# The layer norm of the streamed last stage: root on VectorE, normalising one step earlier

## Chip, core and metric

The kernel runs on one core of one Trainium2 chip. The metric is the device time of one launch in microseconds (us): 2959.16 us before the change, the median of three runs (2955.97, 2959.16 and 2968.11). About 0.5% of it, some 15 us, is what a measurement of this kernel can tell from no change.

## The reference, cut to what matters

A decoder of four levels; the change touches only the last stage, `L3_ffn`: six layers (DEPTH) over x of 4 x 256 x 128, each of local attention with 16 heads of 64 and a gated feed-forward part behind a layer norm.

```python
def ffn_layer(x, g, bln, W1, b1, W2, b2):
    mu = x.mean(-1, keepdims=True)
    var = ((x - mu) ** 2).mean(-1, keepdims=True)
    xn = (x - mu) / jnp.sqrt(var + 1e-05) * g + bln
    hg = xn @ W1 + b1
    a, gate = jnp.split(hg, 2, -1)
    return a * jax.nn.gelu(gate, approximate=False) @ W2 + b2
for i in range(DEPTH):
    x = attn_layer(shift_tokens(x), Wqkv[i], q_scale[i], k_scale[i], Wo[i]) + x
    x = ffn_layer(shift_tokens(x), ln_g[i], ln_b[i], W1[i], b1[i], W2[i], b2[i]) + x
```

`shift_tokens` moves the upper 64 columns of each row one token down.

## The kernel before

The stage is one block, `stream`, that runs all six layers without a barrier. Its unit is the **job**, one batch of one layer: JOBS = 24 jobs, each of 8 (PER) **groups**, a group being a pair of heads. The program walks through **ticks** s, and every engine has its own loop over the same ticks. In each tick the engines do one step each for groups of different age: TensorE scores group s (L2076, L2081), turns q and k of group s + 1 (L2093), turns the probabilities of group s - 2 (`flip`, L2102) and sums the values of group s - 3 (L2199); VectorE takes the row maxima (L2376) and ScalarE the exponentials (L2233). What a job needs once is put at fixed ticks after its first group. I count a job's ticks from there: the output projection stands at OUT = 12, the shifted late rows at LATE = 13, the turn of the normalised rows at ZT = 15, the gates at 16, and so on to DOWN = 19. So the norm of job n runs while the groups of the next job are worked on. In even ticks TensorE projects q of a future job (L2054), in odd ones k (L2063) and v (L2068), up to tick 183 of the whole stage (its groups end at tick 191).

Each engine takes its instructions strictly in the order in which the code's loops write them. So the place of a step in an engine's loop decides what stands behind it. The places that matter here:

- VectorE, tick 13, last: the copy of the late half into z (`late_moved`, L2424). Tick 14: first the reciprocal of the sums of the group before (L2359, POOL waits for it), then `bn_stats`, `bn_aggr` and two small operations that leave variance + eps in `ln_sum` (L2371) and minus the mean in `ln_shift` (L2372), and only then the row maxima of the tick's group (L2376). Later in the tick come two products for the rotation (L2346, L2352), the copy of the turned probabilities, and in even ticks the copy of the next group's `qk_T`. 
- POOL, tick 14: shares out the probabilities (L2305), scales the next group (L2315), then the inverse root of the norm (`inverse_root`, L1861 to L1867: 14 small operations that wait for each other, by Newton steps from a bit trick) and `ln_shift` times `ln_inv` (L2325), then L2297, which adds the two parts of the rotation.
- ScalarE, tick 13, last: the lower half of z (`low_moved`, L2247). Tick 15, last: it waits for `ln_shifted`, normalises the two tiles of z (L2259), waits for their transpose and moves it to `znT` (L2263). The first thing of every tick is the copy of the values that TensorE has summed into `rope` (`stored`, L2217), since they share PSUM bank 7 with the v projection.
- TensorE, tick 15: k projection, v projection, scores, turn, flip, then the two transposes of z (L2143, waits for `normed`), then the values.

The v projection waits for that copy at the top of the same tick on ScalarE:

```python
until(pe, stored, min(G, s - VALUES))
until(pe, v_copied, u)
nc.tensor.matmul(v_bank, own, w_qkv[:, 2 * INNER + c * BANK:2 * INNER + (c + 1) * BANK],
```

Of the kernel before, what the change touches and what calls it, by code (L numbers as in the profile page):

```python
# [16 lines left out]
I32 = mybir.dt.int32  # L17
ALU = mybir.AluOpType
# [3 lines left out]
P = 128  # L22
# [3 lines left out]
QT = N // P  # L26
# [18 lines left out]
LN_EPS = 1e-5  # L45
# [59 lines left out]
def decoder(nc, a, out):  # L105
    ctx = ExitStack()
    with ctx:
        signal = Signals(nc, ctx, [(name, 1) for name in AHEAD] + [(name, STEPS_AHEAD) for name in AHEAD_BY_STEPS])
# [10 lines left out]
        def copy(engine, dst, src, scale=1.0):  # L119

            if engine == "act":
                return nc.scalar.activation(dst, src, ACT.Copy, scale=scale)  # L122
            if isinstance(scale, float) and scale == 1.0:
                return nc.vector.tensor_copy(dst, src)  # L124
            return nc.vector.tensor_scalar(dst, src, scale, None, ALU.mult)

        def affine(engine, dst, src, scale, bias):

            if engine == "act":
                return nc.scalar.activation(dst, src, ACT.Identity, bias=bias, scale=scale)  # L130
            return nc.vector.tensor_scalar(dst, src, scale, bias, ALU.mult, ALU.add)
# [3 lines left out]
        xin = sb("xin", [P, NT, D])  # L135
        z = sb("z", [P, NT, D])
        xnT = sb("xnT", [P, T])
        stats = sb("stats", [P, MT, 6])
# [1647 lines left out]
        def l3_ffn():  # L1786
            sub = ExitStack()
            with sub:
                def sbl(name, shape, dt=F32):
                    return sub.enter_context(nc.sbuf_tensor("net_" + name, shape, dt))  # L1790
# [17 lines left out]
                ln_sum, ln_inv, ln_shift, ln_temp = sbl("ln_sum", [P, QT]), sbl("ln_inv", [P, QT]), sbl("ln_shift", [P, QT]), sbl("ln_temp", [P, 3, QT])  # L1808
# [14 lines left out]
                with nc.Block() as block:  # L1823
# [8 lines left out]
                    def _(pool):  # L1832
# [4 lines left out]
                       (head_sums, head_inv, head_temp), (ln_sum, ln_inv, ln_shift, ln_temp), (qk_T, probs, flat_p, maxima, sums, inverse, window16),  # L1837
# [32 lines left out]
        def stream(p, GT, rows, weights, tables, heads_norm, ln, softmax, ffn):  # L1870
# [18 lines left out]
            ln_sum, ln_inv, ln_shift, ln_temp = ln  # L1889
# [9 lines left out]
            half = D // 2  # L1899
# [15 lines left out]
            measured, gathered, spread_in = signal("net_measured", 2 * JOBS), signal("net_gathered", 2 * JOBS), signal("net_spread", 2 * JOBS)  # L1915
            ln_rooted, normed = signal("net_ln_rooted", ROOT_OPS * JOBS), signal("net_normed", 2 * JOBS)
# [13 lines left out]
            def at_tick(s, lag, every, count):  # L1930

                i, rest = divmod(s - lag, every)
                return i if rest == 0 and 0 <= i < count else None

            def job(n):
                return n // B, n % B
# [15 lines left out]
            def half_cols(c):  # L1952
                return slice(c * BANK, (c + 1) * BANK)
# [20 lines left out]
            with ps("bank", [P, 8, BANK]) as bank, nc.Block() as block:  # L1974
# [229 lines left out]
                def _(act):  # L2204
# [7 lines left out]
                    for s in TICKS:  # L2212
# [9 lines left out]
                        if u is not None:  # L2222
                            m, c, t = step_of(u)
                            square(u, 1, k_filled)
                            act.wait_ge(v_filled.sem, v_filled.at(0, u + 1))
                            copy("act", vals[:, m % 3, t, half_cols(c)], v_bank).then_inc(v_copied.sem, 1)
                        g = s
# [14 lines left out]
                        n = at_tick(s, LATE, PER, JOBS)  # L2242
                        if n is not None:
                            l, b = job(n)
                            own = slice(QT * b, QT * (b + 1))
                            act.wait_ge(out_added.sem, out_added.at(0, n + 1))
                            copy("act", z[:, own, 0:half], xin[:, own, 0:half]).then_inc(low_moved.sem, 1)  # L2247
# [5 lines left out]
                        n = at_tick(s, ZT, PER, JOBS)  # L2253
                        if n is not None:
                            l, b = job(n)
                            act.wait_ge(ln_shifted.sem, ln_shifted.at(0, n + 1))
                            for q in range(QT):
                                own = z[:, QT * b + q, :]
                                affine("act", own, own, ln_inv[:, q:q + 1], ln_shift[:, q:q + 1]).then_inc(normed.sem, 1)  # L2259
                            if b == 0:  # L2260
                                act.wait_ge(ffn_in.sem, ffn_in.at(l, FFN_LOADS))
                            act.wait_ge(z_turned.sem, z_turned.at(0, n + 1))
                            affine("act", znT[:, :], spare[:, 0:N], vec[:, 0:1], vec[:, 1:2]).then_inc(z_moved.sem, 1)  # L2263
# [16 lines left out]
                def _(pool):  # L2280
# [19 lines left out]
                    for s in TICKS:  # L2300
# [19 lines left out]
                        n = at_tick(s, LATE + 1, PER, JOBS)  # L2320
                        if n is not None:
                            pool.wait_ge(spread_in.sem, spread_in.at(0, 2 * n + 2))
                            inverse_root(pool, ln_sum[:, :], LN_EPS, ln_inv[:, :], ln_temp, ln_rooted, ROOT_OPS * n)
                            pool.wait_ge(ln_rooted.sem, ln_rooted.at(0, ROOT_OPS * (n + 1)))
                            nc.gpsimd.tensor_tensor(ln_shift[:, :], ln_shift[:, :], ln_inv[:, :], ALU.mult).then_inc(ln_shifted.sem, 1)  # L2325
# [11 lines left out]
                def _(dve):  # L2337
# [16 lines left out]

                    for s in TICKS:
# [4 lines left out]
                        n = at_tick(s, LATE + 1, PER, JOBS)  # L2360
                        if n is not None:
                            l, b = job(n)
                            dve.wait_ge(late_moved.sem, late_moved.at(0, n + 1))
                            dve.wait_ge(low_moved.sem, low_moved.at(0, n + 1))
                            for q in range(QT):
                                nc.vector.bn_stats(stats[:, q, :], z[:, QT * b + q, :]).then_inc(measured.sem, 1)
                            for q in range(QT):
                                dve.wait_ge(measured.sem, measured.at(0, 2 * n + q + 1))
                                nc.vector.bn_aggr(meanvar[:, q, :], stats[:, q, :]).then_inc(gathered.sem, 1)
                            dve.wait_ge(gathered.sem, gathered.at(0, 2 * n + 2))  # L2370
                            nc.vector.tensor_scalar(ln_sum[:, :], meanvar[:, 0:QT, 1], LN_EPS, None, ALU.add).then_inc(spread_in.sem, 1)  # L2371
                            nc.vector.tensor_scalar(ln_shift[:, :], meanvar[:, 0:QT, 0], -1.0, None, ALU.mult).then_inc(spread_in.sem, 1)  # L2372
# [48 lines left out]
                        if n is not None:  # L2421
                            l, b = job(n)
                            dve.wait_ge(late_made.sem, late_made.at(0, n + 1))
                            copy("dve", z[:, QT * b:QT * (b + 1), half:D], spare[:, 0:D].rearrange("p (t d) -> p t d", t=QT)).then_inc(late_moved.sem, 1)  # L2424
                        m = at_tick(s, SHIFT, PER, JOBS)
# [164 lines left out]
```

## Time and profile before

| | |
|---|---|
| median of three runs | 2959.16 us |
| profiled execution, its time | 2968.27 us |
| its span | 2966.2 us |
| busy over the span: TensorE, VectorE, ScalarE, POOL | 2603.8, 1741.8, 1564.3, 1437.3 us |
| mean granted TensorE clock | 0.932 of full speed |
| the streamed stage | from about 1834 us to the end |

The profiled execution is 9.1 us above the median of the runs. Every time stamp below is in us from the start of its span. In a timeline a row gives the start, the duration, the engine, the line, the operation with what it writes and reads, how many instructions are merged in it, and in brackets how long the engine sat idle ahead of it and whose end it awaited. Line numbers are those of the kernel before.

### The profile page before, as it was taken

What the parts mean: (1) busy time and instruction counts of PE and PEld (TensorE: products, weight loads), DVE (VectorE), ACT (ScalarE), POOL (GpSimd) and SP (SyncE); (2) the same over time, 40 slices, a digit from 0 to 9 for tenths busy, and PEclk for the clock granted to TensorE, in tenths of its full rate; (3) what the DMA queues carried; (4) which work ended last, traced back from release to release, by engine and by line L of the source; (5) the groups of instructions that cost most, each with busy time, mean ns of one, the idle gap of its engine ahead of it and who ended that gap; (6) DMA issues with size and microseconds to landing.
All of it is one profiled execution on the core that took longest, in us unless ns stands there. A gap on an engine that the chain in (4) does not pass through costs nothing. (4 is left out here: it accounts for less than half of the span.)

```text
span 2966.2 us, 59262 instructions
## 1 busy us (share of the span) xinstructions
PE 2603.8 (88%) x20009; PEld 1667.5 (56%) x20009; DVE 1741.8 (59%) x3832; ACT 1564.3 (53%) x5035; POOL 1437.3 (48%) x2340
## 2 busy tenths in 40 slices
PE   5999978798989979776689996899999999999996
PEld 3455545465646646454445553566666666666665
DVE  3466656546657645555545555766666667667662
ACT  1465536425747646532245553666665666666653
POOL 0344434203536613300024443877777777877772
PEclk8799998898979989987789998999999999999998
DMA  2000000000000010000000001010101101001000
GB/s 68 1 0 0 0 8 2 12 32 5 2 4 2 1 32 0 5 1 8 2 25 0 0 0 57 15 34 19 30 25 28 33 19 30 26 26 33 19 23 8
DMA packets 45611, 47.14 MB, mean 16 GB/s; under 512 B 11899, under 2 KB 31365, under 8 KB 45382
## 3 DMA queue, kind: packets, MB, share of 16 engines
q1 hardware_dynamic: 45382, 44.18, 5.3%
q8 instruction: 133, 2.18, 0.3%
q14 instruction: 96, 0.79, 0.1%
HBM read 31.05 MB, written 0.52 MB: 11 GB/s over the span
## 5 line engine op out<-in xcount | busy, mean ns | idle before, releaser
L1022 POOL TENSOR_TENSOR l_probs<-l_probs,rowinv 128x512 f32<-128x512 f32 (+2 forms) x256 | 192.7, 774 | 573.1 <-DVE rowinv L1034 572.4
L1042 DVE TENSOR_REDUCE negmax<-scores 128x1 f32<-128x508 f32 (+4 forms) x512 | 213.1, 468 | 222.3 <-PE scores L919 180.2
L2233 ACT ACTIVATE net_probs<-bank,net_negmax 128x96 f32<-128x96 f32 x768 | 251.7, 340 | 170.9 <-DVE net_negmax L2376 170.7
L2376 DVE TENSOR_REDUCE net_negmax<-bank 128x4 f32<-128x384 f32 x192 | 107.1, 558 | 328.7 <-PE bank L2081 328.0
L1022 POOL TENSOR_TENSOR lora_probs<-lora_probs,rowinv 128x508 f32<-128x508 f32 (+1 forms) x256 | 149.7, 618 | 254.6 <-DVE rowinv L1034 254.6
L2297 POOL TENSOR_TENSOR net_rope<-net_rope,net_sin_parts 128x512 f32<-128x512 f32 x192 | 244.1, 1271 | 9.8 <-DVE net_sin_parts L2352 9.7
L2305 POOL TENSOR_TENSOR net_probs<-net_probs,net_inverse 128x384 f32<-128x384 f32 x192 | 158.8, 827 | 160.8 <-DVE net_inverse L2359 160.8
L987 ACT ACTIVATE l_probs<-scores,negmax 128x512 f32<-128x512 f32 (+2 forms) x256 | 139.7, 551 | 167.9 <-DVE negmax L1042 167.1
L124 DVE COPY turned<-flip 128x512 f32<-128x512 f32 (+3 forms) x280 | 163.3, 583 | 74.0 <-PE flip L946 64.6
L2315 POOL TENSOR_TENSOR net_rope<-net_rope,net_head_inv 128x512 f32<-128x512 f32 x192 | 201.3, 1049 | 0.0
L734 DVE TENSOR_REDUCE negmax<-scores 128x2 f32<-128x256 f32 (+2 forms) x192 | 157.9, 823 | 65.7 <-PE scores L642 36.3
L919 PE MATMUL scores<-kT,qM 64*128 64x512 f32 (+2 forms) x768 | 189.6, 571 | 7.4 <-ACT kT L122 4.1
L2081 PEld LDWEIGHTS bank<-net_qk_T 64*64 64x64 f32 x3072 | 128.3, 138 | 112.6 <-issue 112.6
L987 ACT ACTIVATE lora_probs<-scores,negmax 128x508 f32<-128x508 f32 (+1 forms) x256 | 117.9, 472 | 132.1 <-DVE negmax L1042 131.3
L122 ACT ACTIVATE turned<-flip 128x512 f32<-128x512 f32 (+3 forms) x280 | 143.5, 513 | 58.8 <-PE flip L656 48.8
L969 PE MATMUL heads<-turned,V 128*64 128x256 f32 (+1 forms) x1280 | 166.3, 381 | 2.0 <-ACT turned L122 1.4
L2081 PE MATMUL bank<-net_qk_T 64*64 64x96 f32 (+1 forms) x3072 | 165.5, 249 | 0.0
L2210 ACT ACTIVATE net_squares<-bank 128x512 f32<-128x512 f32 x192 | 115.0, 599 | 93.3 <-PE bank L2054 53.8
L2233 ACT ACTIVATION_READ_ACCUMULATOR net_probs<-bank,net_negmax 128x1 f32 x768 | 156.0, 203 | 0.0
L719 POOL TENSOR_TENSOR cross_probs<-cross_probs,rowinv 128x1024 f32<-128x1024 f32 x64 | 119.9, 1895 | 66.2 <-DVE rowinv L729 66.2
L2346 DVE TENSOR_TENSOR net_rope<-bank,net_cos_table 128x512 f32<-128x512 f32 x192 | 131.0, 682 | 12.1 <-ACT net_squares L2210 11.9
L2093 PE MATMUL bank<-ident,net_rope 128*128 128x128 f32 x768 | 129.7, 293 | 8.6 <-POOL net_rope L2315 8.6
(426 smaller groups left out, 6492.1 us busy)
## 6 DMA issues: line engine op xcount, KB each, us to landing
net_w_qkv<-in_L_ffn_Wqkv SPq DMA_DIRECT2D x12, 768.0 KB, 5.5
net_vals_between<-net_vals SPq DMA_DIRECT2D x48, 192.0 KB, 2.5
net_w_out<-in_L_ffn_Wo SPq DMA_DIRECT2D x6, 512.0 KB, 4.3
net_vals_between<-net_vals SPq DMA_DIRECT2D x48, 64.0 KB, 1.9
moe_w<-in_L_ffn_w13T SPq DMA_DIRECT2D x8, 256.0 KB, 2.7
net_w<-in_L_ffn_W SPq DMA_DIRECT2D x6, 341.0 KB
moe_w<-in_L_ffn_w2T SPq DMA_DIRECT2D x8, 128.0 KB, 2.3
ctx_tok<-in_ctx SPq DMA_DIRECT2D x1, 768.0 KB, 6.6
```

Of the source, the lines that this page charges most:

```text
L124: return nc.vector.tensor_copy(dst, src)
L734: nc.vector.tensor_reduce(negmax[:, c:c + 2], scores[:, 2 * half:2 * half + 2, 0:nk], AX.X, ALU.max, negate=True).then_inc(maxed.sem, 1)
L919: last = nc.tensor.matmul(scores[:, 2 * qt + h, 0:nk], qM[rows, 0, t * P:(t + 1) * P], kT[rows, k0:k0 + nk], start=True, stop=cross)
L969: last = nc.tensor.matmul(heads[rows, q0 * P:QT * P], V[:, v0 + j, rows], turned[:, 2 * p + h, c0:c0 + w], start=(j == 0), stop=(j == part ...
L987: last = nc.scalar.activation(pr[:, slot(g, qt, h), k0:k1], scores[:, 2 * qt + h, k0:k1], ACT.Exp, bias=negmax[:, u * tail + w:u * tail + ...
L1022: last = nc.gpsimd.tensor_tensor(own, own, rowinv[:, u * tail + w:u * tail + w + 1].to_broadcast([P, k1 - k0]), ALU.mult)
L1042: last = nc.vector.tensor_reduce(negmax[:, u * tail + w:u * tail + w + 1], scores[:, 2 * qt + h, k0:k1], AX.X, ALU.max, negate=True)
L2081: last = nc.tensor.matmul(bank[rows_of(h), 4 + g % 2, first:(w + 1) * KEYS], qk_T[rows_of(h), g % 2, 0, w * QB:(w + 1) * QB], qk_T[rows_of ...
L2233: last = nc.scalar.activation(prob_blocks(g)[:, w, :], score_blocks(g)[:, w, :], ACT.Exp, bias=maxima[:, g % 4, w:w + 1], accum_out=sums[: ...
L2297: nc.gpsimd.tensor_tensor(own, own, sin_parts[:, (2 * u + s) % 4, :], ALU.add).then_inc(added.sem, 1)
L2305: nc.gpsimd.tensor_tensor(prob_blocks(g), prob_blocks(g), part, ALU.mult).then_inc(shared.sem, 1)
L2315: nc.gpsimd.tensor_tensor(own, own, factor.to_broadcast([P, 4, 2, DH]), ALU.mult).then_inc(scaled.sem, 1)
```

## The change

Four edits, all in `stream`. (1) On VectorE the statistics stand right behind the late copy at the end of tick 13 instead of behind the reciprocal in tick 14. (2) The inverse root leaves POOL (14 operations and L2325) and is written for VectorE as 11 operations that wait for each other (an addition goes into a `scalar_tensor_tensor`), and one that makes `ln_shift`; the two small operations L2371 and L2372 go. (3) ScalarE's copy of the lower half of z moves within tick 13 from its end to ahead of the exponentials. (4) ScalarE normalises z at the end of tick 14 (ZT - 1) instead of tick 15; the transposes on TensorE and the move to `znT` stay in tick 15.

```diff
@@ -2224,6 +2225,12 @@
                             square(u, 1, k_filled)
                             act.wait_ge(v_filled.sem, v_filled.at(0, u + 1))
                             copy("act", vals[:, m % 3, t, half_cols(c)], v_bank).then_inc(v_copied.sem, 1)
+                        n = at_tick(s, LATE, PER, JOBS)
+                        if n is not None:
+                            l, b = job(n)
+                            own = slice(QT * b, QT * (b + 1))
+                            act.wait_ge(out_added.sem, out_added.at(0, n + 1))
+                            copy("act", z[:, own, 0:half], xin[:, own, 0:half]).then_inc(low_moved.sem, 1)
                         g = s
                         if 0 <= g < G:
                             act.wait_ge(maxed.sem, maxed.at(0, g + 1))
@@ -2239,24 +2246,21 @@
 
                             until(act, scored, g - 1)
                             copy("act", qk_T[:, g % 2, :, :].rearrange("p s n -> p (s n)"), turn_bank).then_inc(copied["act"].sem, 1)
...
-                        n = at_tick(s, LATE, PER, JOBS)
-                        if n is not None:
-                            l, b = job(n)
-                            own = slice(QT * b, QT * (b + 1))
-                            act.wait_ge(out_added.sem, out_added.at(0, n + 1))
-                            copy("act", z[:, own, 0:half], xin[:, own, 0:half]).then_inc(low_moved.sem, 1)
                         m = at_tick(s, SHIFT, PER, JOBS)
                         if m is not None:
...
-                        n = at_tick(s, ZT, PER, JOBS)
+                        n = at_tick(s, ZT - 1, PER, JOBS)
                         if n is not None:
                             l, b = job(n)
                             act.wait_ge(ln_shifted.sem, ln_shifted.at(0, n + 1))
                             for q in range(QT):
                                 own = z[:, QT * b + q, :]
                                 affine("act", own, own, ln_inv[:, q:q + 1], ln_shift[:, q:q + 1]).then_inc(normed.sem, 1)
+                        n = at_tick(s, ZT, PER, JOBS)
+                        if n is not None:
+                            l, b = job(n)
                             if b == 0:
                                 act.wait_ge(ffn_in.sem, ffn_in.at(l, FFN_LOADS))
                             act.wait_ge(z_turned.sem, z_turned.at(0, n + 1))
@@ -2317,12 +2321,6 @@
...
-                        n = at_tick(s, LATE + 1, PER, JOBS)
-                        if n is not None:
-                            pool.wait_ge(spread_in.sem, spread_in.at(0, 2 * n + 2))
-                            inverse_root(pool, ln_sum[:, :], LN_EPS, ln_inv[:, :], ln_temp, ln_rooted, ROOT_OPS * n)
-                            pool.wait_ge(ln_rooted.sem, ln_rooted.at(0, ROOT_OPS * (n + 1)))
-                            nc.gpsimd.tensor_tensor(ln_shift[:, :], ln_shift[:, :], ln_inv[:, :], ALU.mult).then_inc(ln_shifted.sem, 1)
                         u = at_tick(s, PROJ + 1, 2, S)
                         if u is not None:
                             add_parts(u, 0)
@@ -2352,24 +2350,30 @@
...
+                    def root_of_variance(dve, n):
+
+                        lower, y, t = ln_temp[:, 0, :], ln_temp[:, 1, :], ln_temp[:, 2, :]
+                        done = [LN_OPS * n]
+
+                        def then(ins):
+                            done[0] += 1
+                            ins.then_inc(ln_rooted.sem, 1)
+                            dve.wait_ge(ln_rooted.sem, ln_rooted.at(0, done[0]))
+                        then(nc.vector.tensor_scalar(lower, meanvar[:, 0:QT, 1], LN_EPS, -0.5, ALU.add, ALU.mult))
+                        then(nc.vector.tensor_scalar(y.bitcast(I32), lower.bitcast(I32), -0.5, ROOT_MAGIC, ALU.mult, ALU.add))
+                        for r in range(3):
+                            then(nc.vector.tensor_tensor(t, y, y, ALU.mult))
+                            then(nc.vector.tensor_tensor(t, t, lower, ALU.mult))
+                            then(nc.vector.scalar_tensor_tensor(y if r < 2 else ln_inv[:, :], t, 1.5, y, ALU.add, ALU.mult))
+                        assert done[0] == LN_OPS * (n + 1)
+
+                        nc.vector.scalar_tensor_tensor(ln_shift[:, :], meanvar[:, 0:QT, 0], -1.0, ln_inv[:, :], ALU.mult, ALU.mult).then_inc(ln_shifted.sem, 1)
+
                     for s in TICKS:
                         g = s - 1
                         if 0 <= g < G:
...
-                        n = at_tick(s, LATE + 1, PER, JOBS)
-                        if n is not None:
-                            l, b = job(n)
-                            dve.wait_ge(late_moved.sem, late_moved.at(0, n + 1))
-                            dve.wait_ge(low_moved.sem, low_moved.at(0, n + 1))
-                            for q in range(QT):
-                                nc.vector.bn_stats(stats[:, q, :], z[:, QT * b + q, :]).then_inc(measured.sem, 1)
-                            for q in range(QT):
-                                dve.wait_ge(measured.sem, measured.at(0, 2 * n + q + 1))
-                                nc.vector.bn_aggr(meanvar[:, q, :], stats[:, q, :]).then_inc(gathered.sem, 1)
-                            dve.wait_ge(gathered.sem, gathered.at(0, 2 * n + 2))
-                            nc.vector.tensor_scalar(ln_sum[:, :], meanvar[:, 0:QT, 1], LN_EPS, None, ALU.add).then_inc(spread_in.sem, 1)
-                            nc.vector.tensor_scalar(ln_shift[:, :], meanvar[:, 0:QT, 0], -1.0, None, ALU.mult).then_inc(spread_in.sem, 1)
                         g = s
                         if 0 <= g < G:
                             dve.wait_ge(scored.sem, scored.at(0, g + 1))
@@ -2422,6 +2426,15 @@
...
+                            dve.wait_ge(late_moved.sem, late_moved.at(0, n + 1))
+                            dve.wait_ge(low_moved.sem, low_moved.at(0, n + 1))
+                            for q in range(QT):
+                                nc.vector.bn_stats(stats[:, q, :], z[:, QT * b + q, :]).then_inc(measured.sem, 1)
+                            for q in range(QT):
+                                dve.wait_ge(measured.sem, measured.at(0, 2 * n + q + 1))
+                                nc.vector.bn_aggr(meanvar[:, q, :], stats[:, q, :]).then_inc(gathered.sem, 1)
+                            dve.wait_ge(gathered.sem, gathered.at(0, 2 * n + 2))
+                            root_of_variance(dve, n)
                         m = at_tick(s, SHIFT, PER, JOBS)
```

VectorE from the late copy of z (end of tick 13) to the row maxima of tick 14. `bank` is PSUM, `net_negmax` the maxima, `net_inverse` the reciprocals. Before:

```order
L124 COPY z<-bank 128x2x64 [waits net_late_made]
L2359 RECIPROCAL net_inverse<-net_sums 128x4 [waits net_exped]
L2366 BN_STATS stats<-z 128x6 [waits net_low_moved,net_late_moved]
L2369 BN_AGGR meanvar<-stats 128x2 [waits net_measured] x2
L2371 TENSOR_SCALAR net_ln_sum<-meanvar 128x2 [waits net_gathered]
L2372 TENSOR_SCALAR net_ln_shift<-meanvar 128x2
L2376 TENSOR_REDUCE net_negmax<-bank 128x4 [waits net_scored]
```

And changed (the three lines L2365 to L2367 stand three times in a row, the last time into `net_ln_inv`):

```order
L124 COPY z<-bank 128x2x64 [waits net_late_made]
L2432 BN_STATS stats<-z 128x6 [waits net_low_moved,net_late_moved]
L2435 BN_AGGR meanvar<-stats 128x2 [waits net_measured] x2
L2362 TENSOR_SCALAR net_ln_temp<-meanvar 128x2 [waits net_gathered]
L2363 TENSOR_SCALAR net_ln_temp<-net_ln_temp 128x2 [waits net_ln_rooted]
L2365 TENSOR_TENSOR net_ln_temp<-net_ln_temp 128x2 [waits net_ln_rooted]
...
L2367 SCALAR_TENSOR_TENSOR net_ln_inv<-net_ln_temp 128x2 [waits net_ln_rooted]
L2370 SCALAR_TENSOR_TENSOR net_ln_shift<-meanvar,net_ln_inv 128x2 [waits net_ln_rooted]
L2376 RECIPROCAL net_inverse<-net_sums 128x4 [waits net_exped]
L2380 TENSOR_REDUCE net_negmax<-bank 128x4 [waits net_scored]
```

Twelve small operations now stand ahead of the reciprocal and of the row maxima, where five instructions stood ahead of the maxima.

ScalarE from tick 14's exponentials to the end of tick 15. `xnT` is the input of a future job's projections, `net_rope` the copy called `stored`. Before:

```order
L2233 ACTIVATE net_probs,net_sums<-bank,net_negmax 128x96 x3
L122 ACTIVATE xnT<-bank 64x256 [waits net_shift_made]
L122 ACTIVATE net_rope<-bank 128x2x128 [waits net_summed]
L2210 ACTIVATE net_squares<-bank 128x512 [waits net_reduced,net_k_filled]
...
L122 ACTIVATE net_qk_T<-bank 128x512 [waits net_scored,net_turned]
L130 ACTIVATE z<-z,net_ln_shift,net_ln_inv 128x128 [waits net_ln_shifted]
L130 ACTIVATE z<-z,net_ln_shift,net_ln_inv 128x128
L130 ACTIVATE net_znT<-bank,net_layer_cols 128x256 [waits net_z_turned]
```

And changed:

```order
L2240 ACTIVATE net_probs,net_sums<-bank,net_negmax 128x96 x3
L122 ACTIVATE xnT<-bank 64x256 [waits net_shift_made]
L130 ACTIVATE z<-z,net_ln_shift,net_ln_inv 128x128 [waits net_ln_shifted]
L130 ACTIVATE z<-z,net_ln_shift,net_ln_inv 128x128
L122 ACTIVATE net_rope<-bank 128x2x128 [waits net_summed]
L2211 ACTIVATE net_squares<-bank 128x512 [waits net_reduced,net_k_filled]
...
L122 ACTIVATE net_qk_T<-bank 128x512 [waits net_scored,net_turned]
L130 ACTIVATE net_znT<-bank,net_layer_cols 128x256 [waits net_z_turned]
```

The two normalising instructions moved from behind tick 15's exponentials to ahead of tick 15's copy into `net_rope`.

## Rows read from the trace of the kernel before

**Rows 1.** Waits of TensorE, 1905 to 2966: total us, times, longest us.

```profile
PE bank L2143 <- ACT z L130: 62.0, 24, 6.6
PE bank L2068 <- ACT net_rope L122: 8.3, 22, 0.5
```

**Rows 2.** Timeline of TensorE: tick 15 of a job, and the transposes one job on.

```profile
2518.49 1.02 PE L2068 MATMUL bank<-net_w_qkv,xnT 128*128 128x512 f32 x2
...
2523.87 0.44 PE L2143 MATMUL bank<-ident,z 128*128 128x128 f32 x2 [2.42 <-ACT z L130]
...
2568.39 0.44 PE L2143 MATMUL bank<-ident,z 128*128 128x128 f32 x2 [2.41 <-ACT z L130]
```

**Rows 3.** Timeline of ScalarE, ticks 14 and 15 of that job.

```profile
2516.40 0.34 ACT L2233 ACTIVATE net_probs<-bank,net_negmax 128x96 f32<-128x96 f32 x1 [0.93 <-DVE net_negmax L2376]
...
2517.94 0.38 ACT L122 ACTIVATE net_rope<-bank 128x256 f32<-128x256 f32 x1
...
2522.93 0.89 ACT L130 ACTIVATE z<-z,net_ln_shift,net_ln_inv 128x128 f32<-128x128 f32 x2
```

**Rows 4.** Timelines of ScalarE and TensorE, tick 19: a late copy and v.

```profile
2540.59 0.40 ACT L122 ACTIVATE net_rope<-bank 128x256 f32<-128x256 f32 x1
...
2541.04 1.12 PE L2068 MATMUL bank<-net_w_qkv,xnT 128*128 128x512 f32 x2 [0.38 <-ACT net_rope L122]
```

**Rows 5.** Timeline of VectorE, end of tick 13 and tick 14.

```profile
2513.85 0.28 DVE L124 COPY z<-bank 128x128 f32<-128x128 f32 x1
...
2514.37 0.48 DVE L2366 BATCH_NORM_STATS2 stats<-z 128x6 f32<-128x128 f32 x2
...
2515.10 0.17 DVE L2371 TENSOR_SCALAR net_ln_sum<-meanvar 128x2 f32<-128x2 f32 x1
2515.18 0.23 DVE L2372 TENSOR_SCALAR net_ln_shift<-meanvar 128x2 f32<-128x2 f32 x1
2515.80 0.56 DVE L2376 TENSOR_REDUCE net_negmax<-bank 128x4 f32<-128x384 f32 x1 [0.40 <-PE bank L2081]
...
2518.07 0.68 DVE L124 COPY net_qk_T<-bank 128x512 f32<-128x512 f32 x1
```

**Rows 6.** Timeline of VectorE: instructions that wait for the one ahead.

```profile
2939.09 0.29 DVE L124 COPY z<-bank 128x128 f32<-128x128 f32 x1 [1.04 <-PE bank L2126]
2939.42 0.49 DVE L2366 BATCH_NORM_STATS2 stats<-z 128x6 f32<-128x128 f32 x2
...
428.97 0.17 DVE L286 TENSOR_TENSOR spread<-meanvar 128x8 f32<-128x8 f32 x1
429.17 0.17 DVE L289 SCALAR_TENSOR_TENSOR spread<-meanvar,spread 128x8 f32<-128x8 f32 x1
```

**Rows 7.** Timeline of POOL, tick 14 of the job of rows 5.

```profile
2515.12 0.26 POOL L1867 TENSOR_TENSOR net_head_inv<-net_head_temp 128x32 f32<-128x32 f32 x1
2515.34 1.27 POOL L2297 TENSOR_TENSOR net_rope<-net_rope,net_sin_parts 128x512 f32<-128x512 f32 x1
```

**Rows 8.** Timelines of POOL and VectorE: one job off the pattern, one without POOL.

```profile
2423.90 1.28 POOL L2297 TENSOR_TENSOR net_rope<-net_rope,net_sin_parts 128x512 f32<-128x512 f32 x1
...
2424.02 1.18 DVE L2371 TENSOR_SCALAR net_ln_sum<-meanvar 128x2 f32<-128x2 f32 x1
...
2914.11 0.16 DVE L2372 TENSOR_SCALAR net_ln_shift<-meanvar 128x2 f32<-128x2 f32 x1
```

**Rows 9.** TensorE by stretch: length, busy (instructions), granted clock, DMA share, GB/s.

```profile
2202.00:2205.50 3.50, 3.48 (x16) 0.51 0.02 5
...
2523.90:2527.40 3.50, 3.50 (x38) 1.00 0.57 186
```

**Rows 10.** Timeline of TensorE: the transposes of two other successive jobs.

```profile
2202.03 0.69 PE L2143 MATMUL bank<-ident,z 128*128 128x128 f32 x2 [2.41 <-ACT z L130]
...
2248.11 0.44 PE L2143 MATMUL bank<-ident,z 128*128 128x128 f32 x2 [2.41 <-ACT z L130]
```

**Rows 11.** Timeline of ScalarE: the normalising of the last job.

```profile
2944.71 0.88 ACT L130 ACTIVATE z<-z,net_ln_shift,net_ln_inv 128x128 f32<-128x128 f32 x2 [6.31 <-POOL net_ln_shift L2325]
```

More of the change, by code:

```diff
@@ L1807, in l3_ffn @@
                 head_temp = sbl("head_temp", [P, 3, QT * 2 * HB])
-                ln_sum, ln_inv, ln_shift, ln_temp = sbl("ln_sum", [P, QT]), sbl("ln_inv", [P, QT]), sbl("ln_shift", [P, QT]), sbl("ln_temp", [P, 3, QT])
+                ln_inv, ln_shift, ln_temp = sbl("ln_inv", [P, QT]), sbl("ln_shift", [P, QT]), sbl("ln_temp", [P, 3, QT])
                 qk_T = sbl("qk_T", [P, 2, 2, N])
@@ L1836, in l3_ffn @@
                 stream(p, GT, (rope, sin_parts, squares, vals, mid), (w_qkv, w_out, w1, w2, vec), (qk_rows, sines, cosines, sin_table, cos_table),
-                       (head_sums, head_inv, head_temp), (ln_sum, ln_inv, ln_shift, ln_temp), (qk_T, probs, flat_p, maxima, sums, inverse, window16),
+                       (head_sums, head_inv, head_temp), (ln_inv, ln_shift, ln_temp), (qk_T, probs, flat_p, maxima, sums, inverse, window16),
                        (late, znT, gelu, acts))
@@ L1888, in stream @@
             head_sums, head_inv, head_temp = heads_norm
-            ln_sum, ln_inv, ln_shift, ln_temp = ln
+            ln_inv, ln_shift, ln_temp = ln
             qk_T, probs, flat_p, maxima, sums, inverse, window16 = softmax
@@ L1914, in stream @@
             low_moved, late_made, late_moved = signal("net_low_moved", JOBS), signal("net_late_made", JOBS), signal("net_late_moved", JOBS)
-            measured, gathered, spread_in = signal("net_measured", 2 * JOBS), signal("net_gathered", 2 * JOBS), signal("net_spread", 2 * JOBS)
-            ln_rooted, normed = signal("net_ln_rooted", ROOT_OPS * JOBS), signal("net_normed", 2 * JOBS)
+            measured, gathered = signal("net_measured", 2 * JOBS), signal("net_gathered", 2 * JOBS)
+            LN_OPS = 11
+            ln_rooted, normed = signal("net_ln_rooted", LN_OPS * JOBS), signal("net_normed", 2 * JOBS)
             ln_shifted = signal("net_ln_shifted", JOBS)
```

## The prediction

> **What bounds the kernel now.** I read the waits of TensorE first, since it is the engine that hardly ever rests in this stage. One row stands out: the two transposes of the normalised rows wait 62.0 us in 24 jobs for ScalarE's normalising; the next wait in the change's reach, v behind the copy into `net_rope`, sums to 8.3 us [rows 1]. The timeline of one job shows it: v starts at 2518.49, and the transposes of tick 15 at 2523.87 after 2.42 us idle [rows 2]. All 22 jobs that still have projections beside them (jobs 0 to 21) repeat this within a few hundredths; 7 of the 20 intervals from job 0 to job 20 are 44.5 us, as from 2523.87 to 2568.39. So whatever the change adds or takes on TensorE's path counts 22 times, and all else in the job can be read from this one.
>
> Why is the normalising late? It stands behind tick 15's exponentials on ScalarE and starts at 2522.93 [rows 3]. The edits aim at this wait, and taken alone they remove it. The question is what is late next.
>
> **The root on VectorE.** The statistics can start once the late copy has landed. In the last job, where nothing stands between, they start 0.33 us after the copy's start (2939.09 to 2939.42) [rows 6]; here that gives 2513.85 + 0.33 = 2514.18. Their end leads to the first small operation 0.73 us later (2514.37 to 2515.10) [rows 5]: 2514.91. A small operation of VectorE that waits for the one ahead follows it by 0.20 us (428.97 to 429.17) [rows 6]. Alone, eleven of them take 2.20 us, so `ln_shift` would start at 2517.11. Behind it the reciprocal follows at the spacing of two small operations that don't wait, 0.08 (2515.10 to 2515.18) [rows 5], and the row maxima 0.20 later, taken as for a waiting one: 2517.39, against 2515.80 before. So without anything else in its way the chain puts the maxima of tick 14 back by 1.59 us. The 0.40 us for which VectorE sat idle there before [rows 5] are used up in this.
>
> **What POOL does meanwhile.** POOL runs L2297 from 2515.34 for 1.27 us [rows 7], in the middle of the chain. The job in which a small VectorE operation fell into L2297 shows what that does: L2371 started at 2424.02, 0.12 us behind L2297's start, and took 1.18 us instead of 0.17; it ended 1.30 us after L2297 began [rows 5, 8]. L2372 took 0.23 us where POOL's L1867 ran beside it, and 0.16 us with POOL at rest [rows 5, 7, 8]. So VectorE's small operation is held until POOL's has ended. The row is of an operation with one input in SBUF; most in the new chain have two, and no row shows such a one beside POOL. Bounds: nothing (they pass) and the full hold. I take the full hold, as the only row that is near.
>
> The Trainium skill says the same of both kinds (SBUF — State Buffer, "SBUF: two separate sides"): VectorE and GpSimd share a pair of ports, held as an exclusive lock for a whole instruction, and an operation with two SBUF inputs asks for it just as one in a two-port mode does. The row of L2371 agrees for one input. By this rule the held chain below follows; if two inputs passed, the sum would be that of the chain alone.
>
> Worked out: the first operation runs at 2514.91, the second at 2515.11, beside L1867, and takes 0.07 more; the third is due at 2515.38, when L2297 has begun. It ends at 2515.34 + 1.30 = 2516.64, the fourth starts at 2516.67, and the twelfth (`ln_shift`) 8 x 0.20 later at 2518.27. There is no second hold, since POOL's next step is the sharing out of the probabilities, which waits for the reciprocal that now stands behind the chain. Reciprocal and maxima follow at 2518.35 and 2518.55: **the maxima are 2.75 us late**.
>
> **From the maxima to TensorE.** Tick 14's exponentials follow the maxima by 0.60 us (2515.80 to 2516.40) [rows 3, 5], and everything behind them on ScalarE moves by 2.75 us too. The copy into `net_rope` at the top of tick 15 ended at 2517.94 + 0.38 = 2518.32 [rows 3]. It moves by 2.75, and by the two normalising instructions that now stand ahead of it: 0.89 us for the pair [rows 3], 0.80 from start to start of what follows. It ends at 2521.87. The v projection of tick 15 waits for just this copy, because both use PSUM bank 7. A late copy in tick 19 shows the price: it ended at 2540.99, v started at 2541.04 after a wait [rows 4]. So v starts at 2521.92 instead of 2518.49: **3.43 us of wait ahead of v in place of 2.42 us ahead of the transposes**. Net +1.01 us for a job, x 22 = +22.2 us.
>
> What else could be late is covered by this wait: VectorE's copy of `qk_T`, which the scores behind v need, ended at 2518.75 [rows 5] and now ends at 2521.50, ahead of v. The transposes of tick 15 find z ready, as ScalarE normalises ahead of the copy that v waited for.
>
> **Edits with one answer.** ScalarE's lower half of z moves into the 0.93 us in which ScalarE waited for the maxima of tick 13 (the same idle time stands in tick 14's row [rows 3]); the copy of twice as many columns takes 0.40 us [rows 4], so it fits and costs nothing; were there no such idle time it would cost up to 0.4 us a job. The 15 small POOL operations that go free some 4 us of POOL in a job, on an engine that nothing waits for here: nothing. Job 22 has no projections beside it, so no v to wait: its transposes' wait goes, and part of it comes back as a wait for `qk_T`; between 0 and 2.4 us gain, I take 1. In the last job nothing hides the chain: from the statistics (2939.42) to the normalising (2944.71) [rows 6, 11] it was 5.29 us and is now 0.73 + 2.20 + 0.22 = 3.15, a gain of 2.1.
>
> **The clock.** In 13 of those 20 intervals the job takes 46.1 us or more (2202.03 to 2248.11) [rows 10]: behind the idle time the granted clock is 0.51 of full speed for 3.5 us, the lower of the two levels (1.2 GHz), where in the other jobs it stays at 1.00, after the same idle time [rows 9]. A fall costs 46.08 - 44.52 = 1.56 us. With 3.43 us idle instead of 2.42 I take the share of falls to rise in proportion, from 13 in 20 to 18: 5 x 1.56 = +7.8 us. Bounds: none more, and all 20 with two of them in the rest (+14); a fall below the 13 would take up to 20 away.
>
> **The sum** is made on the profiled execution: 2968.3 + 22.2 - 1 - 2.1 + 7.8 = 2995.2 us. It lies 9.1 above the median, so the prediction is 2986.1, +0.9%.
>
> **Rivals.**
> (a) *Two-input operations pass POOL, or the chain meets it otherwise.* Then the maxima are 1.59 us late, v waits 2.27 us against 2.42, net -0.15 x 22 = -3.3; with -3.1 for the end and no more falls the median gives 2952.8. With fewer falls down to 2940. For it: no row shows a two-input operation held. Against it: L2297 covers 1.27 us of a 2.2 us chain, and the second operation is of the kind that was held. The break-even hold is 0.29 us a job (0.15 + 3.1/22); the rest of the 1.16 us is loss. 14%.
> (b) *The wait simply goes*, because ScalarE's copy is not what v waits for or comes in time: -2.4 x 22 - 3, and with it the falls behind it, -20: 2892 on the profiled execution, 2883 on the median, 2903 if the falls stay. Against it is the order of ScalarE's loop itself and the row of tick 19. 4%.
> (c) *Chain slower than 0.20 us a step.* POOL's 16 steps (to the normalising) took 5.29 - 0.73 us in the last job, 0.285 us each [rows 6, 11]; at that spacing on VectorE the eight steps behind the hold come 0.7 us later: +15 us, 3001, and with every job falling up to 3010. The row against it is VectorE's own, 0.20. 7%.
> (d) *The forecast*: hold and displaced wait, 2972 to 3001 by the falls, 75%.
>
> **Chances and range.** Half a per cent, 15 us, is what a measurement tells from no change: faster means under 2944.4, slower over 2974.0. Slower: (d) but for a tenth that lies below 2974, and (c): 0.73. Faster: (b) and a quarter of (a), with something for a pattern of falls that breaks up: 0.08. The same: the rest, 0.19. The range reaches from the lower edge of (d) some way towards (a), 2964, to its upper edge with a little of (c), 3002.
>
> **What would show it.** Right: the transposes' wait is near 0 for jobs 0 to 21, and a wait of v for `net_rope` of about 3.4 us stands in its place, 22 times, some 75 us in all; one small operation in each chain takes over 1 us; the maxima of tick 14 start about 4.7 us behind the late copy of z; more of the intervals are long ones. Wrong: a chain of twelve operations of 0.2 us without a long one in it (then a), or v starting within 0.1 us of the end of k (then b). What would upset the number while the steps hold is the count of falls, and an earlier or later POOL.

## The result, and the profile after

The changed kernel takes 3002.04 us (median of four runs, 2993.98 to 3007.65) against 2959.39 (2955.97 to 2968.11): ratio 1.0129, 95% interval 1.0108 to 1.0150. It is slower by 1.3%. The profiled execution took 3006.04 us with a span of 3004.2, 38.0 more than before.

The waits of TensorE from 1905 us to the end (total, times, longest), which answer [rows 1]:

```profile
PE bank L2069 <- ACT net_rope L122: 70.5, 43, 3.0
...
PE bank L2144 <- ACT z L130: 4.4, 1, 4.4
```

The transposes (now L2144) wait in the last job alone. The v projection (now L2069) waits for ScalarE's copy into `net_rope` instead: 22 times 2.85 to 2.98 us, and 21 times the 0.3 to 0.4 us of tick 19 that stood there before.

VectorE's timeline of one job, from the late copy of z to tick 14's maxima, answers [rows 5]:

```profile
2531.60 0.28 DVE L124 COPY z<-bank 128x128 f32<-128x128 f32 x1
2531.91 0.48 DVE L2432 BATCH_NORM_STATS2 stats<-z 128x6 f32<-128x128 f32 x2
...
2532.65 0.17 DVE L2362 TENSOR_SCALAR net_ln_temp<-meanvar 128x2 f32<-128x2 f32 x1
...
2533.06 0.16 DVE L2365 TENSOR_TENSOR net_ln_temp<-net_ln_temp 128x2 f32<-128x2 f32 x1
2533.25 1.14 DVE L2366 TENSOR_TENSOR net_ln_temp<-net_ln_temp 128x2 f32<-128x2 f32 x1
2534.42 0.16 DVE L2367 SCALAR_TENSOR_TENSOR net_ln_temp<-net_ln_temp 128x2 f32<-128x2 f32 x1
...
2535.79 0.16 DVE L2370 SCALAR_TENSOR_TENSOR net_ln_shift<-meanvar,net_ln_inv 128x2 f32<-128x2 f32 x1
...
2535.95 0.53 DVE L2380 TENSOR_REDUCE net_negmax<-bank 128x4 f32<-128x384 f32 x1
```

And POOL's, over the same time, answers [rows 7]:

```profile
2533.10 1.27 POOL L2301 TENSOR_TENSOR net_rope<-net_rope,net_sin_parts 128x512 f32<-128x512 f32 x1
2536.12 0.83 POOL L2309 TENSOR_TENSOR net_probs<-net_probs,net_inverse 128x384 f32<-128x384 f32 x1 [1.76 <-DVE net_inverse L2376]
```

One of the twelve small operations is long, the one that starts while POOL's addition runs (2533.10 to 2534.37), and it ends at 2534.39. All others take 0.16 to 0.17 us at a spacing of 0.20. The maxima come 4.35 us behind the late copy's start, where it was 1.95: 2.40 us later. The same long operation stands in each of the 22 jobs that have projections beside them.

ScalarE and TensorE behind it answer [rows 3] and [rows 2]:

```profile
2536.52 0.34 ACT L2240 ACTIVATE net_probs<-bank,net_negmax 128x96 f32<-128x96 f32 x1 [3.30 <-DVE net_negmax L2380]
...
2538.06 0.88 ACT L130 ACTIVATE z<-z,net_ln_shift,net_ln_inv 128x128 f32<-128x128 f32 x2
2538.83 0.38 ACT L122 ACTIVATE net_rope<-bank 128x256 f32<-128x256 f32 x1
```

```profile
2535.28 1.12 PE L2064 MATMUL bank<-net_w_qkv,xnT 128*128 128x512 f32 x2
2539.26 2.08 PE L2069 MATMUL bank<-net_w_qkv,xnT 128*128 128x512 f32 x2 [2.86 <-ACT net_rope L122]
...
2544.72 0.60 PE L2144 MATMUL bank<-ident,z 128*128 128x128 f32 x2
...
2592.51 0.60 PE L2144 MATMUL bank<-ident,z 128*128 128x128 f32 x2
```

v starts 0.05 us behind the end of the copy, at 2539.26. It takes 2.08 us instead of 1.02, and the transposes, which wait for nothing, come at 2544.72. A job takes 47.79 us, and so do all 20 intervals (47.77 to 47.82). The granted clock by stretch (columns as in [rows 9]) shows why v is slow:

```profile
2536.40:2539.20 2.80, 0.00 (x0) 0.85 0.00 0
2539.20:2544.90 5.70, 5.64 (x28) 0.50 0.23 52
2544.90:2548.40 3.50, 3.50 (x39) 0.96 0.71 212
```

The clock has fallen before the idle time is over, and it stays at the lower level (1.2 GHz) through the 5.7 us of work from v to behind the transposes. Before, it was low for 3.4 us, as in [rows 9], and not in every job.

The span's 38.0 us in parts: the 20 intervals between the transposes of jobs 0 and 20 sum to 955.9 us against 911.5, +44.4; what comes ahead of them is 3.8 us shorter (the stage's first projection starts at 1825.0 instead of 1830.3, behind stages that the change does not touch, and the first job loses 1.5 of this again), and what follows is 2.6 us shorter: in it job 21, which still has a v to wait for, takes 1.8 us more, and what comes behind job 21 takes 4.4 us less.

### The profile page after: what moved, and what is told of

It reads as the page before. It is cut to its first block and busy times, and to the rows that moved or that the text cites. A ratio compares the mean times of both kernels' runs of the same rounds, so it can differ in the third digit from the quotient of the medians.

```text
span 3004.2 us, 59142 instructions
## 1 busy us (share of the span) xinstructions
PE 2635.6 (88%) x20009; PEld 1688.0 (56%) x20009; DVE 1800.3 (60%) x4072; ACT 1557.8 (52%) x5035; POOL 1364.5 (45%) x1980
## 5 line engine op out<-in xcount | busy, mean ns | idle before, releaser
L2082 PEld LDWEIGHTS bank<-net_qk_T 64*64 64x64 f32 x3072 | 134.6, 143 | 119.2 <-issue 119.2
L2069 PE MATMUL bank<-net_w_qkv,xnT 128*128 128x512 f32 x192 | 123.4, 729 | 70.5 <-ACT net_rope L122 70.5
L2082 PE MATMUL bank<-net_qk_T 64*64 64x96 f32 (+1 forms) x3072 | 173.3, 257 | 0.0
L2094 PE MATMUL bank<-ident,net_rope 128*128 128x128 f32 x768 | 136.5, 304 | 8.4 <-POOL net_rope L2319 8.4
```

The lines of the kernel that those rows point to most:

```text
L2082: last = nc.tensor.matmul(bank[rows_of(h), 4 + g % 2, first:(w + 1) * KEYS], qk_T[rows_of(h), g % 2, 0, w * QB:(w + 1) * QB], qk_T[rows_of ...
```

## Experiments

The runs came in two groups on two chips, where the kernel before took 2971.65 us (one run) and 2960.74 (eight runs, 2957.15 to 2967.01). Within a group times can be compared; across them I compare the intervals between the transposes of successive jobs, which repeat within 0.2 us in most runs where the clock does not fall. Of these, 20 are counted in each run, from the transposes of job 0 on. Counts of falls are those of one profiled execution of each kernel.

**The hold.** POOL's addition of tick 13 is put off to tick 14:

```diff
-                        if u is not None:
+                        if u is not None and at_tick(s, LATE, PER, JOBS) is None:
                             add_parts(u, 0)
                         u = at_tick(s, PROJ + 2, 2, S)
                         if u is not None:
+                            if at_tick(s, LATE + 1, PER, JOBS) is not None:
+                                add_parts(u, 0)
                             add_parts(u, 1)
```

> The changed kernel with one POOL instruction moved: the addition of the rotation's parts that POOL runs in tick 13, beside VectorE's chain, comes in tick 14, behind the sharing out and the scaling. Theory H (VectorE's fourth small operation took 1.14 us in every job because POOL's addition held the ports): no operation of the chain takes over 0.4 us, the maxima of tick 14 come about 1.0 us sooner, v waits about 1.9 us instead of 2.86, and a job takes 46.8 us or, if the shorter idle time no longer brings the clock down, about 44.3, instead of 47.80. Rival I (the long operation has its cause on VectorE, whatever POOL does): the fourth operation still takes over 1 us and a job 47.8.

Measured: 2948.61 us (one run). VectorE's chain and TensorE's v:

```profile
2501.05 0.16 DVE L2368 TENSOR_TENSOR net_ln_temp<-net_ln_temp 128x2 f32<-128x2 f32 x1
...
2502.61 0.16 DVE L2372 SCALAR_TENSOR_TENSOR net_ln_shift<-meanvar,net_ln_inv 128x2 f32<-128x2 f32 x1
```

```profile
2506.08 1.12 PE L2069 MATMUL bank<-net_w_qkv,xnT 128*128 128x512 f32 x2 [1.89 <-ACT net_rope L122]
```

No operation of the chain is long in any job, though they are the same twelve. v waits 1.89 us, 0.97 less, and a job takes 44.05 us, in 4 of 20 intervals 45.6. So the long operation came from POOL's addition, and the other explanation falls. One small operation held beside one POOL operation cost 3.7 us a job where the clock now stays up (3.4 on the mean of the 20): 1 us by the hold and, as the runs below show, most of the rest by the clock.

**The displaced wait.** ScalarE's normalising goes behind the copy of v in tick 15, into the time in which ScalarE waits for that tick's maxima:

```diff
                             copy("act", vals[:, m % 3, t, half_cols(c)], v_bank).then_inc(v_copied.sem, 1)
+                        n = at_tick(s, ZT, PER, JOBS)
+                        if n is not None:
+                            l, b = job(n)
+                            act.wait_ge(ln_shifted.sem, ln_shifted.at(0, n + 1))
+                            for q in range(QT):
+                                own = z[:, QT * b + q, :]
+                                affine("act", own, own, ln_inv[:, q:q + 1], ln_shift[:, q:q + 1]).then_inc(normed.sem, 1)
...
-                        n = at_tick(s, ZT - 1, PER, JOBS)
```

> The changed kernel with ScalarE's two normalising instructions moved out of the end of tick 14 into tick 15, behind the copy of v and ahead of the exponentials. Theory D (the wait ahead of v is what the maxima's delay and the two normalising instructions add up to): v waits 2.86 - 0.78 = about 2.1 us, the transposes of z still wait for nothing, and a job takes 47.0 us with a fall of the clock and 44.5 without. Rival (v's wait comes from the delayed maxima alone, or the transposes now wait): v waits 2.86 as before, or the transposes' wait is back with over 0.5 us.

Measured: 2933.33 us (one run).

```profile
2585.76 1.12 PE L2069 MATMUL bank<-net_w_qkv,xnT 128*128 128x512 f32 x2 [2.24 <-ACT net_rope L122]
...
2588.67 0.38 PE L2144 MATMUL bank<-ident,z 128*128 128x128 f32 x2
```

v waits 2.24 us, 0.62 less (0.78 expected), the transposes wait for nothing, and all 20 intervals take 44.2 to 44.4 us, with no fall of the clock in any of them. (Job 0, ahead of the first interval, has one, 0.9 us behind the start of its v and after the same 2.24 us of idle time.) From v's start to the transposes it is 2.91 us here and was 5.46 in the changed kernel at the lower clock: **a fall costs 2.55 us there**, where it cost 1.56 in the kernel before.

**The last edit undone** (the root stays on VectorE, ScalarE normalises at the end of tick 15):

```diff
-                        n = at_tick(s, ZT - 1, PER, JOBS)
+                        n = at_tick(s, ZT, PER, JOBS)
```

> The changed kernel with its last edit undone: ScalarE normalises z at the end of tick 15, as before the change. Theory D: both waits stand at once, about 2.1 us ahead of v (the delayed maxima alone) and about 2.4 us ahead of the transposes (normalising behind the exponentials), and a job takes 49 us or more. Rival (v's wait came from the normalising instructions ahead of the copy): v waits under 1 us, and a job is back at 44.5 to 46.1 us.

Measured: 3029.65 us (one run), intervals 46.9 to 51.6 with a mean of 48.4.

```profile
2357.89 1.12 PE L2069 MATMUL bank<-net_w_qkv,xnT 128*128 128x512 f32 x2 [2.24 <-ACT net_rope L122]
...
2363.39 0.44 PE L2144 MATMUL bank<-ident,z 128*128 128x128 f32 x2 [2.43 <-ACT z L130]
```

Both waits stand in one job, as expected. In about half of the jobs the second is 1.44 us, so the mean stays under the 49 that I had written. v's wait of 2.24 us without any normalising ahead of the copy is the delay of the maxima alone.

**The clock.** 16 matmuls fill TensorE's idle time ahead of v in the changed kernel:

```diff
+                            if at_tick(s, ZT, PER, JOBS) is not None:
+                                until(pe, exped, s - 1)
+                                for _ in range(16):
+                                    nc.tensor.matmul(score_bank(s), ident16[:, :], window16[:, :], start=True, stop=True)
                             until(pe, stored, min(G, s - VALUES))
```

> The changed kernel with 16 extra matmuls (window against identity, into the score bank that is free then and overwritten next) between k and v in tick 15, so that TensorE is busy for most of the 2.86 us in which it sat idle. Theory C (the idle time brings the clock down in each of the 20 jobs, and a fall costs about 2.5 us): the granted clock stays at 1.00 behind it, v and what follows take their short times, and a job takes about 45.3 us instead of 47.80, some 50 us for the kernel. Rival (the clock falls for another reason, or what it costs is hidden by the other engines): a job still takes over 47 us.

Measured: 2954.54 us (one run).

```profile
2552.39 2.76 PE L2070 MATMUL bank<-net_window,ident 128*128 128x384 bf16 x16
...
2555.42 1.13 PE L2073 MATMUL bank<-net_w_qkv,xnT 128*128 128x512 f32 x2 [0.26 <-ACT net_rope L122]
...
2558.33 0.38 PE L2148 MATMUL bank<-ident,z 128*128 128x128 f32 x2
```

Nothing comes sooner by the added work, v waits for the same copy, and yet a job takes 45.0 to 45.2 us instead of 47.8. So 2.6 us of the 3.3 that a job lost against 44.52 are the clock, and about 0.65 the wait itself.

The same for the kernel before, 14 matmuls ahead of the transposes' wait:

```diff
+                            if s + 1 < G:
+                                until(pe, exped, s)
+                                for _ in range(14):
+                                    nc.tensor.matmul(score_bank(s + 1), ident16[:, :], window16[:, :], start=True, stop=True)
                             pe.wait_ge(normed.sem, normed.at(0, 2 * n + 2))
```

> The kernel before with 14 extra matmuls (window against identity, into the score bank that is free then and overwritten next) ahead of the transposes of z, so that TensorE is busy for most of its 2.41 us of idle time. Theory C: no fall of the clock behind it, all 20 jobs take 44.5 us (7 of 20 did), some 20 us less than an execution with 13 falls. Rival (falls come from something else than this idle time): the same mix of 44.5 and 46.1 us.

Measured: 2946.04 us (five runs, 2941.21 to 2950.03), ratio 0.9952 (0.9935 to 0.9970). 19 of 20 intervals take 44.5 us, one 45.3, and the granted clock is 1.00 over all 20:

```profile
1925.00:2816.00 891.00, 876.61 (x8001) 1.00 0.10 28
```

The 45.3 is no fall but the job of [rows 8], in which L2297 (here L2300) held a statistics operation of VectorE, 1.15 us here; the kernel before has it too, as an interval of 46.9 us. Matmuls that compute nothing make the kernel before half a per cent faster, by the falls alone.

**Both moves** together, the addition later and the normalising behind v:

> The changed kernel with both of the moves that were tried one by one: POOL's addition of tick 13 comes in tick 14, and ScalarE normalises behind the copy of v in tick 15. Theory D with H: the parts add up, v waits 2.86 - 0.97 - 0.62 = about 1.3 us, the transposes wait for nothing, and a job without a fall of the clock takes 44.52 - 2.42 + 1.4 = 43.5 us: at 20 such jobs some 2915 us, 1.5% under the kernel before. Rival (another wait takes over below 44 us a job, such as VectorE's copy of qk_T or the transposes' wait): a job stays at 44.0 to 44.4 and that wait shows with over 0.4 us.

Measured: 2915.16 us (four runs, 2911.19 to 2921.42), ratio 0.9848 (0.9825 to 0.9871).

```profile
2313.03 1.13 PE L2069 MATMUL bank<-net_w_qkv,xnT 128*128 128x512 f32 x2 [1.11 <-ACT net_rope L122]
...
2315.94 0.38 PE L2144 MATMUL bank<-ident,z 128*128 128x128 f32 x2
```

v waits 1.1 to 1.2 us, a job takes 43.3 us in all 20 intervals, and no other wait has taken over.

**Two Newton steps** instead of three in VectorE's root (a little less exact), with both moves:

```diff
-                        for r in range(3):
+                        for r in range(2):
```

> As the kernel with both moves, and with two Newton steps instead of three in VectorE's root, so that three of the twelve small operations are gone (the root is a little less exact). Theory D: 3 x 0.2 = 0.6 us less delay of the maxima, all of it off v's wait: a job takes 0.6 us less than with three steps, 13 us for the kernel. Rival (the wait ahead of v is no longer what the chain's length sets): under 0.2 us a job.

Measured: 2899.89 us (four runs, 2897.35 to 2904.16), ratio 0.9798 (0.9778 to 0.9817). v's wait falls by another 0.58 us to 0.53, and a job takes 42.7 us:

```profile
2303.60 1.13 PE L2069 MATMUL bank<-net_w_qkv,xnT 128*128 128x512 f32 x2 [0.53 <-ACT net_rope L122]
```

Three small operations of VectorE are worth 15 us of the kernel. The length of the chain passes straight through the maxima, the exponentials and the copy to TensorE.

**Had the root to move at all?** The kernel before, its root on POOL, with the normalising alone moved behind the copy of v:

> The kernel before (root on POOL, statistics in tick 14) with ScalarE's normalising in tick 15 moved behind the copy of v and ahead of the exponentials. If the root's place on POOL is what makes z late (ln_shifted comes at the end of POOL's root, 4 us after the statistics, whatever ScalarE does): the transposes still wait about 2.2 us, and a job takes 44.5 us or more. Rival (only the order of ScalarE made z late, and the root need not have moved): the transposes' wait falls under 1 us and a job under 43.5 us.

Measured: 2948.91 us (one run), most intervals 44.28. ScalarE's timeline:

```profile
2503.43 0.60 ACT L122 ACTIVATE net_vals<-bank 128x512 f32<-128x512 f32 x1 [0.26 <-PE bank L2068]
2506.58 0.88 ACT L130 ACTIVATE z<-z,net_ln_shift,net_ln_inv 128x128 f32<-128x128 f32 x2 [2.56 <-POOL net_ln_shift L2328]
```

ScalarE is free 2.56 us before POOL's root has ended; the transposes still wait 2.18 us. So the root's place on POOL made z late too, and moving it from there was right. I had expected `ln_shifted` 4 us after the statistics. It comes 7.4 us after them (from 2499.14, the end of the operation that makes `ln_sum`, to 2506.55), because the root starts only at 2502.36, behind the sharing out and the scaling. An earlier place for the root in POOL's own loop would therefore be another way to have z sooner. It was not tried. What costs in the change is where it put the root and the normalising.

## The prediction, point by point

**What bounds the kernel; the wait that goes.** Right. The transposes' wait is gone in all jobs but the last, and the wait ahead of v stands in its place, for the reason given: PSUM bank 7 and the order of ScalarE's loop.

**The hold beside POOL.** Right in its kind: one operation of each chain, held to the end of POOL's addition. So an operation with two SBUF inputs is held just as one with one input, which no row before showed; the rule that I had drawn on from the Trainium skill (SBUF — State Buffer, "SBUF: two separate sides") agrees with 1.14 us here and with 0.16 where POOL's addition is moved away. (The addition that [rows 7] put down to tick 14 is the one of POOL's tick 13: with that one put off, the hold is gone.) The size was a little too large: the fourth operation was held, not the third, since the small holds of 0.07 us that I had added beside POOL's root did not show (0.17 for both first operations), and reciprocal and maxima followed each other by 0.08 us instead of 0.20. The maxima are 2.40 us late, not 2.75.

**From the maxima to v.** Right, by that smaller amount: v is pushed back by 3.02 us, not 3.43 (the 2.86 that the row shows run from k's end, 0.16 later than v's old start). As the transposes' 2.42 us go, a job without falls would lose about 0.65 us, by the filled run, against my +1.01: 22 jobs make 14 us of loss instead of 22.

**The clock** is the step that failed in size. I took +7.8 us, from a share of falls in proportion to the idle time and the price of one fall before, 1.56 us. The share went to all 20, and a fall costs 2.55. The 20 intervals account for it: 13 falls of 1.56 us before are 20 us, 20 of 2.55 are 51, together +31 instead of +7.8. The price goes with how long the clock stays low and meets work. Stretches of the changed kernel, of the run with the addition later, and two of the run with the root on POOL (columns as in [rows 9]):

```profile
2538.40:2545.20 6.80, 5.94 (x29) 0.50 0.22 47
```

```profile
2150.40:2153.80 3.40, 3.32 (x17) 0.50 0.00 0
```

```profile
2236.90:2243.70 6.80, 6.40 (x38) 0.51 0.00 0
...
2284.70:2288.10 3.40, 3.40 (x17) 0.51 0.00 0
```

In the changed kernel the clock falls 0.8 to 0.9 us before v starts and stays low for 6.8 us, 5.9 of them with work, in each of the 20 jobs. In the kernel before it fell at the start of the transposes [rows 9] or 1.7 us behind it (at 2065.5, transposes at 2063.8), stayed low for 3.4 us either way and cost 1.56. With the addition later it falls as v starts, stays low for 3.4 us and costs 1.6. With the root on POOL the first of the two falls shown comes 0.3 us before the transposes, stays 6.8 us and costs 3.0; the second comes 0.2 us behind their start, stays 3.4 us and costs 1.6. What makes a low stretch the longer one is not shown; of the falls told here, the long ones are those that came 0.3 us or more before the idle time ended.

The proportion was wrong altogether: with 2.24 us of idle time (the normalising behind v) none of the 20 intervals has a fall, with 1.89 (the addition later) 4 have, with 2.18 (root on POOL) 4, with 2.41 before 13, with 2.86 all. So the length of one wait does not set the share. Nor do the wait and its place in the job together: within one run they are alike in every job, and with the addition later only every fifth interval has a fall. What else takes part was not tried.

**Edits with one answer, and the end.** What comes behind job 21 is 4.4 us shorter (predicted 3.1: the 1 us taken for job 22 and the 2.1 of the last job); the last transposes wait 4.39 us where they waited 6.58. ScalarE's earlier copy of z cost nothing that shows, and POOL's gain was worth nothing by itself: VectorE's reciprocal now makes it wait.

**The sum.** 26.9 us were predicted on the profiled execution, 37.8 came (2968.27 to 3006.04): the wait too large by 8, the clock too small by 23, the rest, 4 the other way, lies for the most part ahead of the streamed stage, where nothing was changed. The median came out 16 us above the prediction and at the upper edge of its range. That it came so near is in part luck: two errors of opposite sign offset each other, and with the predicted wait beside the measured falls it would have been 23 us above the prediction, outside its range. The forecast of +0.9% rests on the displaced wait (+22 us) more than on the clock (+7.8); in the runs it is the other way round (14 and 31). The rivals: (a), that two-input operations pass POOL, falls by the long operation; (b) by the wait ahead of v; (c) by the spacing of 0.20.

## To carry to other kernels

Before moving a step ahead on an in-order engine, read what stands behind the new place: here the first thing behind the normalising freed the PSUM bank that TensorE wanted next, and the place behind the copy of v, 2 us later, cost nothing that shows. A chain of small VectorE operations should run while GpSimd waits: one instruction of 1.27 us beside it added 1 us to it here, and moving that instruction by one tick took the 1 us away. And count the clock with every wait of TensorE: with both moves the same edit makes the kernel 1.5% faster instead of 1.3% slower, and a good half of that difference lies in falls that no longer come.

## What the runs showed of the hardware

A fall of the clock has no one price: about 1.6 us where it was low for 3.4 us, and 2.55 or 3.0 where it was low for 6.8 us, having begun 0.3 to 0.9 us before the idle time ended (in the run with the root on POOL the intervals are 45.86 and 47.24 against 44.28). Idle time of 2.24 us in each job brought none in 20 intervals, and 1.89 us brought four. Filling an idle time of 2.41 us with 14 useless matmuls gave 0.5%. And a VectorE operation on 128x2 elements whose inputs both lie in SBUF took 1.14 us beside a GpSimd operation, seven times its 0.16.
